# Routed experts of a token tower: each expert's last two tiles as one group of 256 rows

## The chip, the cores and the metric

One core of a Trainium2 chip runs the whole kernel in one launch. The metric is the device time of one execution in microseconds. The kernel before takes 499.87 us (median of 3 runs, 499.44 to 500.29). In one expert's work TensorE (PE) multiplies, ScalarE (ACT) applies GELU and rounds, VectorE (DVE) gates and forms remainders, GpSimd (POOL) issues indirect transfers, and SyncE (SP) issues plain ones.

## The reference, cut to what matters

2048 tokens pass an embedding MLP (256 to 1024 to 256), a two-layer gated recurrence, and a mixture of experts with one shared expert and eight routed ones. Only the last stage is changed in earnest:

```python
def geglu(x, w1, w2, w3):
    return jax.nn.gelu(x @ w1, approximate=False) * (x @ w2) @ w3
B, T, C = x.shape                       # 2048 rows of 256, experts 256 -> 1024 -> 256
xf = x.reshape(-1, C)
shared = geglu(xf, w1s, w2s, w3s)
logits = xf @ Wg
idx = jnp.argmax(logits, axis=-1)
final = jnp.zeros_like(xf)
for e in range(N_EXPERTS):              # 8
    y = geglu(xf, W1[e], W2[e], W3[e])
    final = final + jnp.where((idx == e)[:, None], y, 0.0)
return (shared + final).reshape(B, T, C)
```

With the inputs drawn for this case the argmax sends 144, 240, 444, 241, 337, 200, 293 and 149 tokens to experts 0 to 7 (worked out from the reference itself). In tiles of 128 rows that is 2, 2, 4, 2, 3, 2, 3 and 2, so 20 tiles.

## The kernel before, in words

Every product is made from three: each fp32 operand is split into a rounded high part and the low remainder, and `mm3` (L248 to L252) issues high by high, high by low and low by high. The high part is an ACT copy, the low part a DVE subtraction that waits for it.

The program is one instruction stream for each engine, written out by hand and tied by semaphores. Chunks c = 0 to 31 are the embedding MLP, with the recurrence's units between them; c = 32 to 55 are the first three quarters of the shared expert, in which the router's logits are made (`router_logits`, L598), the rows are ranked, and scattered by expert into `x_sorted` in DRAM (16 indirect transfers, L416). Then come the routed tiles, and c = 56 to 63, the last quarter of the shared expert, with the fetch of the routed rows, the sums and the output.

A routed tile (`routed_tile`, PE L726) is 128 rows. PE turns the 256 columns of the tile (`row_transposes`), then keeps the rows in the array (xTp is the stationary operand) and streams 512 columns of w1 or w2 past them (`up_half`, 24 products). ACT makes GELU, DVE gates into g_buf; both are rows by hidden columns, so PE has to turn them in 8 transposes (`g_transposes`, L719) before the 24 down products of 256 columns. One tile's down products run behind the next one's up products. The expert of a tile is read from a table (`expert_of`, a register load). PE runs 16 tiles in any case (SURE) and up to 7 more in `Fori(SURE, END)` with an `If` (L756, L757), since the number of tiles depends on the routing. When a tile is the first of its expert, ACT and DVE split the next expert's weights during it: three pairs `next_hi` (L948) and `next_lo` (L1348) of 2048 columns each.

POOL stores each finished tile with one indirect transfer (`to_tokens`, L422), each of which waits until the one before has landed. Its loop always has XT = 23 rounds; the rounds past the last real tile store rows that go to a spare place of `y_tokens`. Nothing waits for these but POOL itself, and the program is over when all engines are.

SP zeroes `x_sorted` in 25 transfers (L304) and loads the weights.

Of the kernel before, what the change touches and what calls it, by code (L numbers as in the profile page):

```python
# [5 lines left out]
P = 128  # L6
# [13 lines left out]
def build(nc, idx, codebook, tok_w1, tok_b1, tok_w2, tok_b2, gru_wz, gru_bz, gru_wh, gru_bh,  # L20
# [3 lines left out]
    KD = D // P  # L24
# [9 lines left out]
    XT = TILES + EXPERTS - 1  # L34
    SURE = TILES
    END = XT
# [30 lines left out]
    LOG = {43: 3}  # L67
    LOG_END = {31: 0, 38: 1, 41: 2}
# [10 lines left out]
    x_sorted = nc.dram_tensor("x_sorted", [(XT + 2) * P, D + 1], F32, kind="Internal").ap()  # L79
    y_tokens = nc.dram_tensor("y_tokens", [(TILES + 1) * P, D], F32, kind="Internal").ap()  # L80

    with ExitStack() as ctx:
# [25 lines left out]
        r_qT = region(8)  # L108
        r_stage = region(28)
        r_xh = region(8)  # L110
        r_rows = region(17)
        r_xl = region(4)
        r_xb = region(8)
        r_gelub = region(2)

# [33 lines left out]
        x_row = at("x_row", [P, D], F32, r_xl)  # L149
        y_row = at("y_row", [P, D], F32, r_xl + K)  # L150
        xTp = at("xTp", [P, 2, KD, P], F32R, r_xl + 2 * K)
# [20 lines left out]
        wgs = small("wgs", [P, KD, EXPERTS])  # L172
# [21 lines left out]
        tile_no = small("tile_no", [P, XT, EXPERTS - 1])  # L194
        past = small("past", [P, XT, EXPERTS - 1])
        expert_f = small("expert_f", [P, XT])
        turns = small("turns", [P, END + 1], U16)
        fresh = small("fresh", [P, XT])
# [37 lines left out]
        logit_ps = sem("logit_ps"); logits_taken = sem("logits_taken"); onehot_steps = sem("onehot_steps"); onehot_done = sem("onehot_done")  # L236
        rank_ps = sem("rank_ps"); router = sem("router"); placed = sem("placed"); routed = sem("routed"); scattered = sem("scattered")
        first_row_land = sem("first_row_land"); x_land = sem("x_land"); x_ps = sem("x_ps"); xT_hi = sem("xT_hi"); xT_lo = sem("xT_lo")
        a_ps = sem("a_ps"); b_ps = sem("b_ps"); gelu_done = sem("gelu_done"); g_done = sem("g_done")
        gT_ps = sem("gT_ps"); gT_hi = sem("gT_hi"); gT_lo = sem("gT_lo")  # L240
        tile_done = sem("tile_done"); y_taken = sem("y_taken"); y_stored = sem("y_stored")
        act_turn = sem("act_turn"); fetch_land = [sem(f"fetch_land{b}") for b in range(BLOCKS)]
# [15 lines left out]
        def back_of(engine):  # L258

            engine.wait_ge(routed, 1)  # L260
            return engine.value_load(turns[0:1, END:END + 1], min_val=0, max_val=END - SURE) + SURE

# [18 lines left out]
        def _(sp):  # L281
# [5 lines left out]
            sp.dma_start(wgs[:], wg).then_inc(small_land, 16)  # L287
# [15 lines left out]
            with sp.Fori(0, XT + 2) as j:  # L303
                sp.dma_start(x_sorted[bass.ds(j * P, P), :], zero_row[:]).then_inc(zeroed, 16)  # L304
# [13 lines left out]
            sp.dma_start(x_row[:], x_sorted[0:P, 0:D]).then_inc(first_row_land, 16)  # L318
# [22 lines left out]
            sp.wait_ge(x_land, back * 16 + 16)  # L341
# [14 lines left out]
        def _(pool):  # L356
# [5 lines left out]
            def gather(b):  # L362
                for i in range(BT):
# [13 lines left out]
            pool.wait_ge(pool_const, 4)  # L377
            pool.affine_select(out=before[:], in_=before[:], compare_op=ALU.is_gt, fill=0.0, base=0,
# [4 lines left out]
                      allow_small_or_imprecise_dtypes=True).then_inc(pool_const, 1)  # L383
            pool.iota(tile_no[:], [[1, XT], [0, EXPERTS - 1]], base=0, channel_multiplier=0,
# [36 lines left out]
            def to_tokens(i):  # L421
                pool.indirect_dma_start(  # L422
                    out=y_tokens, out_offset=bass.IndirectOffsetOnAxis(ap=row_ids[:, i:i + 1].bitcast(I32), axis=0),
                    in_=y_row[:], in_offset=None,
# [4 lines left out]
            for i in range(XT):  # L429
                pool.wait_ge(y_taken, i + 1)  # L430
                if i:
                    pool.wait_ge(y_stored, i * 16)
                to_tokens(i)
# [3 lines left out]
        def _(pe):  # L437
# [160 lines left out]
            def router_logits(b):  # L598
# [5 lines left out]
                for i in range(BT):  # L604
                    for k in range(KD):
                        last = pe.matmul(ps[:, FLIP, i * EXPERTS:(i + 1) * EXPERTS], xlT[:, k, i * P:(i + 1) * P],  # L606
                                         wgs[:, k, :], start=(k == 0), stop=(k == KD - 1))
                last.then_inc(logit_ps, 1)

# [8 lines left out]
            def row_transposes(i):  # L618
                if isinstance(i, int) and i == 0:
                    pe.wait_ge(first_row_land, 16)  # L620
                else:
                    pe.wait_ge(x_land, i * 16)
# [829 lines left out]
```

## Time and profile before

| what | value |
|---|---|
| median of 3 runs | 499.87 us |
| the profiled execution | 499.71 us, of which the span of its instructions is 498.0 us |
| PE busy | 490.6 us (99%) |
| DVE busy | 320.2 us (64%) |
| ACT busy | 248.6 us (50%) |
| POOL busy | 71.2 us (14%) |
| first routed up product | 269.56 us |
| last real store of routed rows issued | 465.65 us |

The time outside the span is 499.71 - 498.0 = 1.7 us. A record of a busy engine shows how long its instruction was in flight; since matmuls overlap, what one costs is the distance between starts. Idle time is shown only in front of an instruction, with what ended it. Register and branch instructions are not busy time, but the trace has them by line, as PEldq, ACTq or DVEq.

### The profile page before, as it was taken

How to read it: one execution, taken by the hardware profiler on the slowest of the kernel's cores; microseconds unless marked ns; L12 is line 12 of the kernel's file. 1: busy time of each engine (PE TensorE's matmuls, PEld its weight loads, DVE VectorE, ACT ScalarE, POOL GpSimd, SP SyncE). 2: the span in 40 equal slices, each digit the busy share in tenths (PEclk: the TensorE clock that was granted, in tenths of full speed). 3: DMA queues.
4: the chain of work that ended last, by engine and by line, in shares of the span. 5: the costliest groups of instructions: out<-in, count | busy, mean ns of one | idle time of the engine just before them, and what ended most of it. 6: DMA issues, size and time to landing. Idle time of an engine off the chain costs nothing.

```text
span 498.0 us, 9330 instructions
## 1 busy us (share of the span) xinstructions
PE 490.6 (99%) x2946; PEld 434.0 (87%) x2947; DVE 320.2 (64%) x533; ACT 248.6 (50%) x380; POOL 71.2 (14%) x85
## 2 busy tenths in 40 slices
PE   8999999999999999999999999999999999999997
PEld 7889888888888888988888898898898898898886
DVE  2567768668676778657635866833857477557364
ACT  3776774575653553433433765534554457254321
POOL 4431031011011001103460001011001000101110
PEclk9999999999999999999999999999999999999999
DMA  4999010000000004000454465620546084500352
GB/s 132 325 295 239 7 42 1 1 0 2 1 1 1 1 0 168 3 0 33 138 169 108 155 222 205 201 105 32 195 167 227 21 265 133 193 32 32 108 189 84
DMA packets 22857, 52.70 MB, mean 106 GB/s; under 512 B 6096, under 2 KB 16336, under 8 KB 18864
## 3 DMA queue, kind: packets, MB, share of 16 engines
q1 hardware_dynamic: 17168, 42.39, 26.1%
q0 software_dynamic: 2640, 7.22, 4.0%
q10 hardware_dynamic: 3024, 2.75, 1.8%
q8 instruction: 16, 0.26, 0.2%
q14 instruction: 9, 0.07, 0.0%
HBM read 41.85 MB, written 10.51 MB: 105 GB/s over the span
## 4 chain that ended last, share of the span: by engine, by line
PE 94%; DVE 3%; issue 1%; ACT 1%; DVEq 0%
PE ps L250 28%; PE ps L251 28%; PE ps L252 28%; PE ps L719 4%; PE ps L440 2%; PE ps L606 1%; PE ps L624 1%; PE ps L548 1%; PE ps L595 1%; PE ps L583 1%; DVE stats L1080 1%; DVE v_gate L1111 0%; ACT a_gate L867 0%; ACT t_gate L865 0%; ACT v_gate L869 0%
## 5 line engine op out<-in xcount | busy, mean ns | idle before, releaser
L1015 DVE TENSOR_TENSOR hT<-ps,hT 128x512 fp32r<-128x512 f32 x64 | 43.9, 686 | 34.9 <-ACT hT L818 16.6
L1348 DVE TENSOR_TENSOR w_slots<-stage,w_slots 128x2048 f32 x24 | 54.8, 2287 | 15.2 <-ACT w_slots L948 15.1
L250 PE MATMUL ps<-w_slots,xTp 128*128 (+1 forms) x160 | 64.2, 401 | 0.2
L252 PE MATMUL ps<-w_slots,xTp 128*128 (+1 forms) x160 | 62.5, 391 | 0.0
L251 PE MATMUL ps<-w_slots,xTp 128*128 (+1 forms) x160 | 62.2, 389 | 0.0
L422 POOL DMA_INDIRECT y_tokens<-y_row,row_ids x23 | 22.4, 975 | 198.9 <-DVE y_row L1371 188.4
L250 PE MATMUL ps<-w_slots,gTp 128*128 (+1 forms) x160 | 46.8, 293 | 0.0
L818 ACT ACTIVATE hT<-ps 128x512 fp32r<-128x512 f32 x32 | 19.1, 598 | 54.1 <-DVE ps L1021 48.4
L252 PE MATMUL ps<-w_slots,gTp 128*128 (+1 forms) x160 | 45.3, 283 | 0.0
L251 PE MATMUL ps<-w_slots,gTp 128*128 (+1 forms) x160 | 45.2, 283 | 0.0
L1329 DVE TENSOR_TENSOR g_buf<-ps,gelu_buf 128x512 f32<-128x512 f32 x40 | 26.8, 685 | 28.1 <-PE ps L252 28.1
L948 ACT ACTIVATE w_slots<-stage 128x2048 f32 x21 | 40.3, 1917 | 3.9 <-issue 3.9
L1021 DVE TENSOR_TENSOR ps<-ps,gelub 128x512 f32<-128x512 f32 x32 | 22.3, 697 | 30.9 <-PE ps L252 26.0
L972 ACT ACTIVATE gTp<-ps 128x512 fp32r<-128x512 f32 x40 | 21.7, 595 | 39.0 <-PE ps L719 39.0
L802 ACT ACTIVATE ps<-ps,b 128x512 f32<-128x512 f32 x32 | 21.1, 660 | 36.1 <-PE ps L252 36.0
L964 ACT ACTIVATE gelu_buf<-ps 128x512 f32<-128x512 f32 x40 | 23.9, 597 | 29.7 <-PE ps L252 25.3
L814 ACT ACTIVATE gelub<-ps 128x512 f32<-128x512 f32 x32 | 19.2, 600 | 37.5 <-PE ps L252 36.6
L250 PE MATMUL ps<-w2p,hT 128*128 128x256 f32 x128 | 36.8, 288 | 1.0 <-DVE hT L1015 0.7
L250 PE MATMUL ps<-w_slots,hT 128*128 128x256 f32 x128 | 36.5, 285 | 0.0
L252 PE MATMUL ps<-w_slots,hT 128*128 128x256 f32 x128 | 36.2, 283 | 0.0
L251 PE MATMUL ps<-w_slots,hT 128*128 128x256 f32 x128 | 36.2, 283 | 0.0
L252 PE MATMUL ps<-w2p,hT 128*128 128x256 f32 x128 | 36.2, 283 | 0.0
(183 smaller groups left out, 1289.5 us busy)
## 6 DMA issues: line engine op xcount, KB each, us to landing
stage<-ew_in SPq DMA_DIRECT2D x24, 1024.0 KB, 5.0
x_sorted<-zero_row SPq DMA_DIRECT2D x25, 128.5 KB
x_row<-x_sorted ACTq DMA_DIRECT2D x21, 128.0 KB
stage<-w1s_in SPq DMA_DIRECT2D x2, 1024.0 KB, 8.9
fetched<-y_tokens SPq DMA_DIRECT2D x4, 512.0 KB, 5.3
out_rows<-fetched SPq DMA_DIRECT2D x3, 512.0 KB
first_stage<-tok_w_in SPq DMA_DIRECT2D x1, 1024.0 KB, 4.9
first_stage<-tok_w_in SPq DMA_DIRECT2D x4, 256.0 KB
```

What stands on the lines that cost most here:

```text
L250: pe.matmul(dst, lhs_hi, rhs_hi, start=start, stop=False, skip_group_check=shares_bank)
L251: pe.matmul(dst, lhs_hi, rhs_lo, start=False, stop=False, skip_group_check=shares_bank)
L252: return pe.matmul(dst, lhs_lo, rhs_hi, start=False, stop=stop, skip_group_check=shares_bank)
L422: pool.indirect_dma_start(out=y_tokens, out_offset=bass.IndirectOffsetOnAxis(ap=row_ids[:, i:i + 1].bitcast(I32), axis=0), in_=y_row[:], i ...
L802: act.activation(bank, bank, ACT.Gelu_apprx_tanh, bias=b1[:, c % HC:c % HC + 1]).then_inc(h_gelu, 1)
L948: act.activation(w_slots[:, bass.ds((e & 1) * SLOT + c * WCH, WCH)], stage[:, c, :], ACT.Copy).then_inc(split_hi, 1)
L964: act.activation(gelu_buf[:, n, :], ps[:, 2 * n, :], ACT.Gelu).then_inc(gelu_done, 1)
L972: act.activation(gTp[:, 0, n * BT:(n + 1) * BT, :].rearrange("p c n -> p (c n)"), ps[:, 4 + n, :], ACT.Copy).then_inc(gT_hi, 1)
L1015: dve.tensor_tensor(hT[:, c % RING, 1, :], ps[:, bank, :], f32(hT[:, c % RING, 0, :]), ALU.subtract).then_inc(h_lo, 1)
L1021: dve.tensor_tensor(bank, bank, gelub[:], ALU.mult).then_inc(s_gated, 1)
L1329: dve.tensor_tensor(g_buf[:, n * NB:(n + 1) * NB], ps[:, 2 * n + 1, :], gelu_buf[:, n, :], ALU.mult).then_inc(g_done, 1)
L1348: dve.tensor_tensor(w_slots[:, bass.ds(to + (PART + c * WCH), WCH)], stage[:, c, :], f32(w_slots[:, bass.ds(to + c * WCH, WCH)]), ALU.subt ...
```

## The change: what it does

Each expert's last two tiles (one or both possibly part empty) become a window of 256 rows. In a window the weights are loaded into the array and the 256 rows stream past them (`window_up`, four steps p of 24 products of 256 columns), so that the hidden values come out already turned, and the 8 transposes for each tile go. Tiles ahead of the window, the singles, are worked as before, inside the expert's turn, behind the window's first step. Down products of high rows take the high and the low part of w3 in one product of 512 columns, into two halves of a bank, which DVE adds (`take_tile`, a reduction, in place of the copy); so a tile's down has 8 products of 512 and 8 of 256 columns.

```diff
-    XT = TILES + EXPERTS - 1
+    WINDOW = 2 * P
+    PAIRS = HC // 2
+    MORE = TILES - 2
+    XT = 2 * EXPERTS + MORE
...
-            with sp.Fori(0, XT + 2) as j:
-                sp.dma_start(x_sorted[bass.ds(j * P, P), :], zero_row[:]).then_inc(zeroed, 16)
+            for j in range(XT + 2):
+                sp.wait_ge(h_lo, HC + j * 3 // 4)
+                sp.dma_start(x_sorted[j * P:(j + 1) * P, :], zero_row[:]).then_inc(zeroed, 16)
...
             for i in range(XT):
-                pool.wait_ge(y_taken, i + 1)
+                pool.wait_ge(y_taken, i + 2)
                 if i:
                     pool.wait_ge(y_stored, i * 16)
+                pool.sem_inc(y_free, 1)
                 to_tokens(i)
...
+            def expert(e, odd):
+                count = singles_of(pe, e)
+                s = ahead_of(pe, e)
+                last = last_of(pe, e)
+                pe.wait_ge(split_lo, e * 3 + 5)
+                pe.wait_ge(pair_lo, e + 1)
+                window_up(e, 0, odd)
+                if isinstance(e, int) and e == 0:
+                    chunk_down(AHEAD - 1, 0)
+                    pe.wait_ge(acc_taken, 2 * (2 * BLOCKS - 1))
+                else:
+                    window_down(e * PAIRS, PAIRS - 1, not odd)
+                with pe.If(count > 0):
+                    pe.wait_ge(one_lo, s + e + 1)
+                    single_half(s, 0, odd)
+                    pe.wait_ge(w_lo, e * PAIRS + 1)
+                    single_half(s, 1, odd)
+                    pe.wait_ge(y_taken, s + e * 2 + 1)
+                    one_transposes(s + e + 1)
+                    with pe.Fori(1, MORE) as j:
+                        with pe.If((count - j) > 0):
+                            single_turn(s + j - 1, 0)
+                            ...
+                            single_down(s + j - 1, odd)
+                    single_turn(last, 0)
+                window_up(e, 1, odd)
+                with pe.If(count > 0):
+                    single_turn(last, 1)
+                pe.wait_ge(w_lo, e * PAIRS + 1)
+                window_up(e, 2, odd)
+                pe.wait_ge(one_lo, s + count + e + 1)
+                pair_transposes(e + 1)
+                with pe.If(count > 0):
+                    ...
+                    single_down(last, odd)
+                ...
+                window_down(e * PAIRS + 1, 0, odd)
+                pe.wait_ge(w_lo, e * PAIRS + 2)
+                window_up(e, 3, odd)
+                window_down(e * PAIRS + 2, 1, odd)
+                pe.wait_ge(pair_lo, e + 2)
+                one_transposes(s + count + e + 1)
+                window_down(e * PAIRS + 3, 2, odd)
+
+            pe.wait_ge(pair_lo, 1)
+            one_transposes(0)
             chunk_down(AHEAD - 2, 0)
...
+            def take_tile(done, bank, count=1):
+                dve.wait_ge(tile_done, done)
+                dve.wait_ge(y_free, done)
+                dve.tensor_reduce(y_rows[:, bass.ds(((done + 1) & 1) * D, D)], ps[:, bank, :].rearrange("p (h n) -> p n h", h=2), AX,
+                                  ALU.add).then_inc(y_taken, count)
```

ACT and DVE have an `expert` in the same order, with the same `Fori(1, MORE)` and `If`. On DVE one without singles is: gate 0, the two takes, remainder 0, `next_lo` 0, gate 1, remainder 1, `next_lo` 1, gate 2, remainder 2, the remainder of the next window's rows, gate 3, remainder 3, that of the next single's rows, `next_lo` 2. Window rows and single rows are read ahead into x_pair and x_one. The router's logits are now made with wg in the array (32 columns) and the rows streaming, four tiles side by side in the array's column groups, and turned back by one transpose; and `turns` holds five small tables in place of one entry for each tile.

The loop that leaves tiles out stands on PE before in this form (order of the program; L757 is the `If`, and the rows left out are its body):

```order
L756 UNCONDITIONAL_BRANCH
L756 ISA
L757 COMPARE_AND_BRANCH
...
L757 UNCONDITIONAL_BRANCH
L756 REGISTER_ALU
L756 COMPARE_AND_BRANCH
```

and now inside every expert with singles, between the turning of the next single's rows and the turning of the last single's hidden values:

```order
L683 MATMUL ps<-ident,x_one 128x128 x2
L839 UNCONDITIONAL_BRANCH
L839 ISA
L840 COMPARE_AND_BRANCH
...
L840 UNCONDITIONAL_BRANCH
L839 REGISTER_ALU
L839 COMPARE_AND_BRANCH
```

The same three rows drive a round; the loop of before had 7 rounds once in a program, the one of now has 13 in each expert that has a single.

The end of POOL's stream, before:

```order
L395 TENSOR_SCALAR veps<-mv 128x4
L397 TENSOR_TENSOR rstd<-veps,mhalf 128x4
L409 IOTA xn_73 128x16
L416 DMA x_sorted<-xn_73,pos 3200x257 x16
L422 DMA y_tokens<-y_row,row_ids 2176x256 x23
```

and now:

```order
L440 TENSOR_SCALAR veps<-mv 128x4
L442 TENSOR_TENSOR rstd<-veps,mhalf 128x4
L454 IOTA xn_73 128x16
L461 DMA x_sorted<-xn_73,pos 5888x257 x16
L467 DMA y_tokens<-y_rows,row_ids 2176x256 x30
```

Seven stores more stand at the end of the stream; with 20 real tiles 3 of 23 were spare, and 10 of 30 are.

## Rows read from the trace of the kernel before

**Rows 1.** The page: busy time and chain by engine.
```profile
PE 490.6 (99%) x2946; PEld 434.0 (87%) x2947; DVE 320.2 (64%) x533; ACT 248.6 (50%) x380; POOL 71.2 (14%) x85
...
PE 94%; DVE 3%; issue 1%; ACT 1%; DVEq 0%
```

**Rows 2.** Timeline of PE, one routed tile: start us, duration us, line, operation, count.
```profile
343.60 1.04 PE L719 MATMUL ps<-ident,g_buf 128*128 128x128 f32 x8
344.39 0.47 PE L250 MATMUL ps<-w_slots,xTp 128*128 x1
...
349.95 0.38 PE L624 MATMUL ps<-ident,x_row 128*128 128x128 f32 x2
350.08 0.36 PE L250 MATMUL ps<-w_slots,gTp 128*128 x1
...
353.04 0.49 PE L719 MATMUL ps<-ident,g_buf 128*128 128x128 f32 x3
```

**Rows 3.** Timeline of ACT and DVE, splitting the next expert's weights.
```profile
346.55 1.91 ACT L948 ACTIVATE w_slots<-stage 128x2048 f32 x1
...
348.72 2.29 DVE L1348 TENSOR_TENSOR w_slots<-stage,w_slots 128x2048 f32 x1 [0.54 <-ACT w_slots L948]
350.93 0.68 DVE L1329 TENSOR_TENSOR g_buf<-ps,gelu_buf 128x512 f32<-128x512 f32 x1
351.53 0.41 DVE L1149 TENSOR_TENSOR xTp<-ps,xTp 128x256 fp32r<-128x256 f32 x1
```

**Rows 4.** Timeline of DVE and ACT, one chunk of the shared expert.
```profile
478.17 0.70 DVE L1021 TENSOR_TENSOR ps<-ps,gelub 128x512 f32<-128x512 f32 x1 [0.99 <-PE ps L252]
...
478.90 0.60 ACT L818 ACTIVATE hT<-ps 128x512 fp32r<-128x512 f32 x1 [1.57 <-DVE ps L1021]
...
479.53 0.69 DVE L1015 TENSOR_TENSOR hT<-ps,hT 128x512 fp32r<-128x512 f32 x1 [0.66 <-ACT hT L818]
```

**Rows 5.** PE's register loads of the table, 300 to 440 us: ns min/median/max, first and last start.
```profile
L724 PEldq TENSOR_LOAD <-turns x29: 283/284/424, 304.2 to 436.6; - x29
```

**Rows 6.** Timelines of PE and DVE where the routed tiles begin.
```profile
269.56 0.47 PE L250 MATMUL ps<-w_slots,xTp 128*128 128x512 f32 x1
...
269.05 0.42 DVE L1149 TENSOR_TENSOR xTp<-ps,xTp 128x256 fp32r<-128x256 f32 x1
...
273.28 1.41 DVE L1058 TENSOR_TENSOR res<-ps,res 128x512 f32<-128x512 f32 x2
```

**Rows 7.** PE's loop over left-out tiles, 454 to 458 us: ns, first and last start.
```profile
L756 PEldq COMPARE_BRANCH  x4: 76/208/222, 454.8 to 457.3; - x4
...
L757 PEldq COMPARE_BRANCH  x3: 208/208/208, 455.3 to 456.9; - x3
```

**Rows 8.** Timeline of PE's products at the same place.
```profile
456.76 0.28 PE L252 MATMUL ps<-w_slots,gTp 128*128 x1
457.51 1.09 PE L719 MATMUL ps<-ident,g_buf 128*128 128x128 f32 x8 [0.47 <-issue]
```

**Rows 9.** Timeline of PE at the program's start.
```profile
1.25 7.19 PE L440 MATMUL ps<-zero_row 128*128 128x256 f32 x20 [1.25 <-DVE zero_row L991]
...
9.16 1.03 PE L440 MATMUL ps<-zero_row 128*128 128x256 f32 x4
```

**Rows 10.** Timelines of POOL and SP at the end.
```profile
465.65 0.97 POOL L422 DMA_INDIRECT y_tokens<-y_row,row_ids  x1 [6.29 <-DVE y_row L1371]
468.87 0.98 POOL L422 DMA_INDIRECT y_tokens<-y_row,row_ids  x1 [2.24 <-DMA y_tokens<-y_row,row_ids]
475.87 0.97 POOL L422 DMA_INDIRECT y_tokens<-y_row,row_ids  x1 [6.03 <-DMA y_tokens<-y_row,row_ids]
...
468.05 2.04 SPq L339 DMA_DIRECT2D fetched<-y_tokens  x4
```

**Rows 11.** PE's logit products of one block, and its longest waits in all.
```profile
L606 PE MATMUL ps<-wgs,xlT x16: 170/256/256, 188.1 to 189.7; 128*128 128x8 f32 x16
...
PE ps L250 <- issue: 0.9, 1, 0.9
```

More of the change, by code:

```diff
@@ L702, in up_half, with single_turn, single_down @@
                     last.then_inc(done, 1)
-            def down(i, slot):
+            def single_turn(s, n):
+                pe.wait_ge(g_done, s * 2 + (n + 1))
+                for c in range(HC // NH):
+                    j = n * (HC // NH) + c
+                    last = pe.transpose(ps[:, 4 + n, c * P:(c + 1) * P], g_buf[:, j * P:(j + 1) * P], ident[:])
+                last.then_inc(gT_ps, 1)
+            def single_down(s, odd):
+                side = 0 if odd else 1
                 for c in range(HC):
@@ L712, in down @@
+                    last = pe.matmul(ps[:, 7, 0:D], gTp[:, 1, c, :], w_slots[:, side * SLOT + o:side * SLOT + o + D],
+                                     start=False, stop=c == HC - 1, skip_group_check=True)
                 last.then_inc(tile_done, 1)
-            def g_transposes(i):
-                for n in range(NH):
-                    pe.wait_ge(g_done, 2 * i + n + 1)
-                    for c in range(HC // NH):
-                        j = n * (HC // NH) + c
-                        last = pe.transpose(ps[:, 4 + n, c * P:(c + 1) * P], g_buf[:, j * P:(j + 1) * P], ident[:])
-                    last.then_inc(gT_ps, 1)
@@ L976, in _, with window_gelu @@
-            act.wait_ge(routed, 1)
-            tile(0, second_hi)
-            with act.Fori(1, SURE) as i:
-                routed_tile(i)
-            back = back_of(act)
-            with act.Fori(SURE, END) as i:
-                with act.If((back - i) > 0):
-                    routed_tile(i)
+                    window_rows_hi(0, 0)
+                    single_rows_hi(0)
+            def window_gelu(e, p):
+                act.wait_ge(wa_ps, e * PAIRS + (p + 1))
+                act.activation(gelub[:], ps[:, p % 2 * 2, :], ACT.Gelu).then_inc(w_gelu, 1)
@@ L984, in _ @@
+            act.wait_ge(routed, 1)
+            expert(0, 0)
+            with act.Fori(0, EXPERTS // 2 - 1) as i:
+                expert(i * 2 + 1, 1)
+                expert(i * 2 + 2, 0)
+            expert(EXPERTS - 1, 1)
             for c in range(AHEAD, ALL):
@@ L1339, in routed_tile @@
[L1339 to L1352 removed]
+                    window_rows_lo(0, 0)
@@ new lines, in expert @@
+                window_gated(e, 1)
+                window_lo(e, 1)
+                with dve.If(count > 0):
+                    single_lo(last, 1)
+                next_lo(e, 1, odd)
+                window_gated(e, 2)
+                window_lo(e, 2)
+                window_rows_lo(e + 1, 1 - odd)
+                with dve.If(count > 0):
+                    take_tile(s + count + e * 2, 7)
+                window_gated(e, 3)
+                window_lo(e, 3)
+                single_rows_lo(s + count + e + 1)
@@ L1378, in _ @@
+                next_lo(e, 2, odd)
+            dve.wait_ge(routed, 1)
+            expert(0, 0)
+            with dve.Fori(0, EXPERTS // 2 - 1) as i:
+                expert(i * 2 + 1, 1)
+                expert(i * 2 + 2, 0)
+            expert(EXPERTS - 1, 1)
             back = back_of(dve)
-            with dve.Fori(SURE, END) as i:
-                with dve.If((back - i) > 0):
-                    routed_tile(i, lambda: take_routed(i - 1, 16 * i - 16))
             def finish(b):
```

453 lines of the change are left out of this document (271 added, 182 removed).

## The prediction

> **What bounds the kernel now.** I read the page first: PE is busy 99% of the span and carries 94% of the chain that ended last [rows 1]. So every instruction taken off PE is time, as long as PE finds work in its place, and every new wait of PE is time lost. I then read PE's timeline through one routed tile for the distances between starts, ACT's and DVE's for the steps between two of PE's groups, and last the sequencer's own rows (loops, register loads) and POOL's stream at the end, since the change touches both.
>
> A routed tile goes from 343.60 to 353.04, which is 9.44 us: 8 transposes in 0.79, 24 up products of 512 columns in 5.56 (0.08 of it a seam, so 0.228 each), 2 transposes of rows in 0.13, and 24 down products of 256 columns in 2.96, or 0.12 each [rows 2]. There is no idle time in it.
>
> **The work on the array.** A window is two tiles. Its up products are 4 steps of 24 with 256 columns: 96 x 0.12 = 11.5 us, against 2 x 5.56 = 11.1 before. Its down products are 16 pairs of 512 and 256 columns: 16 x (0.228 + 0.12) = 5.6, against 5.9. Six row transposes at 0.1 are 0.6, a seam or two 0.1. Sum 17.8 against 18.9: 1.1 saved, since 1.6 of transposes go. Eight windows save 8.7, and the four singles 0.1 each through the fused down product. Total **-9**. Were the 256-column products dearer with weights in the array, this would shrink; the down products of before have the same shape and bound it.
>
> **Loops that leave tiles out.** This is the largest term. Experts 2, 4 and 6 have 2, 1 and 1 singles. In each, PE passes Fori(1, 14): 13 rounds, of which 12, 13 and 13 do nothing. The kernel before has the same three driving rows, and left out three rounds at the end: the If's taken branch stands at 455.3 and, two rounds later, at 456.9, so one empty round takes 0.8 us of PE's sequencer; the taken branches alone are 0.208 and about 0.21 [rows 7]. Three rounds and the exit took about 2.7 us, and the array stood still from 456.88 to 457.51, 0.63, because the sequencer had been 2.1 us ahead (its loop end at 454.8, the last queued product at 456.76 + 0.12) [rows 7, 8]. That cover is all there is. So 13 rounds are 10.4 us of sequencer and 12 are 9.6, in all 30.4; less 2.1 ahead in expert 2, and less about 1.4 in experts 4 and 6, where the sequencer has just waited for x_one to land, 25.5 us remain. **+25.5**; between 20 (a full lead and rounds of 0.7) and 31 (no lead). ACT and DVE pass the same loop with branches of their own while PE stands, so theirs lies beside it.
>
> The Trainium skill, Advanced Engine Details and Errata, Control Flow Timing, gives some 108 ns for a compare and branch; by it a round of two would be near 0.4 and the term about 12. Rows 7 show 208 ns for a taken one and 0.8 for the round, and the measurement decides.
>
> **The clock behind these gaps.** PE then stands idle for 7 to 9 us three times, which no stretch of before shows; its longest waits are below 1.5. What the trace shows is the start, before which PE did nothing: 20 products begin at 1.25 and the next group at about 8.3, 0.35 each, where the later ones stand (1.03 - 0.38) / 3 = 0.22 apart [rows 9]. The idle start cost 20 x (0.352 - 0.217) = 2.7 us. I take 2.4 for each gap, **+7**, with 0 and 8 as ends. The Trainium skill, TensorE: Matmul & The Clock Gate, Part 1, says that an idle array falls to 1.2 GHz and returns to 2.4 GHz under load; no row of before shows it after a gap in the middle.
>
> **The chain through ACT and DVE.** For an expert without singles (0, 1, 3, 5, 7) I laid the steps in order. Gate to ACT's copy is 0.73, copy to remainder 0.63, remainder 0.69 [rows 4]; ACT's weight copy to DVE's start 2.17, that one's length to the next start 2.21, a 512-column step 0.60 [rows 3]. From gate 0 at 0: two takes, remainder 0 at 2.2, weights 3.4 to 5.6, gate 1 5.6, remainder 1 7.0, weights 9.0 to 11.2, gate 2, remainder 2 12.6, window rows 13.2 to 13.9, gate 3 about 15.3, remainder 3 16.8, weights 17.4 to 19.6. PE needs 17.8 for the same expert, and wants the next window's rows 13.3 after the end of its first up step. So it waits 0.7 the first time, and in expert 1, which follows another without singles, 1.5 to 2. Behind such a wait the sequencer is no longer ahead, and an expert starts with three table loads in a row, each 0.28 for the load itself [rows 5] and, an estimate, twice that with the register steps behind it: 1.9 against 1.4 of queued products, about 1 us more with the waits. Experts 1, 3, 5, 7: 4.3 of waits for rows less what the load gaps give DVE back, 4 of loads. **+7**; ends 1 and 12. The reduction in take_tile is in no row; a 512-column DVE step of 0.69 [rows 4] and the 256-column one of 0.41 [rows 3] bound it, I take the first, since it reads 512.
>
> **The start of the stage.** Before, PE's first routed product starts at 269.56, when the row remainder (269.05 + 0.42) is just done; ahead of it lies chunk_down(54), 12 x 0.12 = 1.4, so that began at about 268.0 [rows 2, 6]. Now one_transposes(0) stands ahead of chunk_down(54) and waits for the window's rows, 512 columns, so until 269.05 + 0.69 = 269.75: 1.7 us, and behind it come the table loads, 1.8 uncovered. In expert 0 PE also waits for DVE's two sums of res after chunk_down(55), 1.41 [rows 6] and 0.3 to be seen, which another half of up products covered before. **+5**; 2 to 7.
>
> **Small edits.** The logits of a block are 16 products in 1.7 us [rows 11]; now 16 of other shape and one transpose. Between a quarter of it and the same: 0 to -5 in all four blocks. Spreading the zeroing takes DMA load away near 18 to 40 us; PE's longest wait without a cause shown is 0.9 [rows 11]. DVE's copies lie beside PE's down products. Together **-1**, from -5 to +2.
>
> **The end.** POOL's 20 real stores are followed by 10 spare ones instead of 3. A store follows the one before after 3.22 us (465.65 to 468.87), and the one that meets the fetch of 2 MB, issued at 468.05, after 7.0, 3.8 more [rows 10]. Before, the last real one stood 498.0 - 465.65 = 32.35 before the end. Call E the time at which PE's chain would end the span. Now the last two tiles are taken together; relative to the rest of PE's work the first store comes about 0.7 later, at E - 31.6, and eleven more follow: -31.6 + 11 x 3.25 + 3.8 + 0.97 = 9. With something for the output transfers of 512 KB it meets, POOL ends the program at E + 10. **+10**; 6 to 14. Before this chain was covered by the last quarter of the shared expert; with 3 spare ones the last began one interval behind 475.87, near 479.
>
> **Sum.** 498.0 - 9 + 25.5 + 7 + 7 + 5 - 1 = 532.5 for E, 542.5 with the end, 544.2 with the 1.7 outside the span. The profiled execution (499.71) is 0.16 below the median of the runs, so 544.
>
> **Rivals.**
> 1. The clock stays at 2.4 GHz through the gaps: 537. For it: the page never shows less than 9 tenths. Against: the start at half pace. It decides if the products right behind a gap stand 0.12 apart.
> 2. Empty rounds are cheap inside an expert, because the body left out is passed without the long branch, or PE's queue hides them. Then term and clock go: 544 - 32.5 = 511. Against: the rows are the same three and rows 7 have three of three rounds at 208.
> 3. Code has to be fetched again: the body of two experts is far longer than a tile's, and five experts jump over the singles' code. The Trainium skill, Runtime: NRT & Kernel Launch, Instruction fetch mechanics, says a taken branch out of the fetched pages stalls. By rows, the nearest is 0.9, the longest wait of PE without a shown cause [rows 11]; two back jumps and fifteen skips at 0 to 0.9 are up to 15: 552 in the middle.
> 4. The other side, faster: the only thing that counts is the array's work. If PE's sequencer stays far enough ahead that rounds, loads and DVE's chain are all hidden, E is 498 - 9 - 1 = 488, and it becomes faster once POOL's spare stores also cost under 10, as they would if one spare store took 2.3 us in place of 3.22 (E + 0): 490. It decides from a lead of 10 us where rows 7 and 8 show 2.1.
> 5. Spare stores end inside the shared quarter: 534.
>
> **Chances.** Forecast 544: 0.44; rival 1 0.16; rival 2 0.07; rival 3 0.18; rival 5 0.1; rival 4 0.03; the rest, 0.02, ends within 0.2% by chance of signs. A measurement of this kernel tells 0.2% from no change. Range 524 to 560: it holds the forecast with most of its terms' ends, rivals 1, 3 and 5, and leaves out 2 and 4. Slower 0.95, same 0.01, faster 0.04.
>
> **What would show it.** In the profile after: PE idle before the first turn of g_buf behind the inner loop, three times, 7 to 10 us each, with COMPARE_BRANCH rows 0.8 apart; products behind it 0.21 apart for some us; PE waiting for the remainder of xW in experts 1, 3, 5 and 7, and none in 2, 4 and 6; POOL's last store behind the last output sum by about 10 us, and the chain that ended last running through POOL. I am wrong if PE stays above 95% busy, if POOL's last store starts before the last product, or if an expert of two tiles takes clearly more than 20 us.

## The result, and the profile after

The changed kernel takes 545.32 us (median of 4 runs, 544.43 to 546.14) against 499.65 before (498.76 to 500.29) on the same chip: ratio 1.0918, 95% interval 1.0894 to 1.0941. Slower by 9%, at the predicted place (544). The profiled execution has a span of 544.0, where before had 498.0.

The page after: the first line is busy time by engine, the second the granted TensorE clock in 40 slices, the last the chain that ended last. They answer to [rows 1].

```profile
PE 486.6 (89%) x3066; PEld 432.9 (80%) x3067; DVE 332.0 (61%) x540; ACT 248.7 (46%) x381; POOL 76.7 (14%) x91
...
PEclk9999999999999999999999997999699988999985
...
POOLq L93 0%; DMA y_tokens<-y_rows,row_ids 0%; POOLq L467 0%
```

PE has 4 us less of work in flight, but its share of the span fell from 99% to 89%. The clock, 9 in every slice before, dips to 7 and 6, and the end of the program belongs to POOL and no longer to PE (the view takes in only a few us of this chain, so its shares are near 0%). The list of PE's longest waits (line waited with, what ended the wait, us in all, times, longest):

```profile
PE ps L801 <- issue: 24.5, 3, 9.3
PE ps L683 <- DVE xW L1300: 3.3, 5, 1.6
PE ps L271 <- issue: 3.0, 5, 0.8
PE ps L271 <- DVE res L1209: 1.4, 1, 1.4
```

The longest wait of before was 1.3, at the program's start. L801 is the transpose of g_buf behind the inner loop: three waits, one in each expert with singles. PE's sequencer in the first of them, 320 to 340 us (ns min/median/max, first and last start), answers to [rows 7]:

```profile
L839 PEldq COMPARE_BRANCH  x13: 76/208/226, 325.3 to 334.2; - x13
L839 PEldq FUSED_REGOPS  x12: 39/39/51, 325.6 to 333.7; - x12
...
L840 PEldq COMPARE_BRANCH  x12: 208/208/215, 325.7 to 333.8; - x12
```

Twelve taken `If`s start between 325.7 and 333.8: eleven distances of 0.74 us. The loop's last branch starts at 334.2 and the turn behind it at 334.43, so it is PE's own sequencer that the array waits for. The timeline of PE at the same place, and its busy time and clock in stretches there and behind the second loop (columns of the second fence: stretch, length, busy time of PE, PEld, DVE, ACT and POOL with instructions, PEclk, DMA share, GB/s):

```profile
328.10 0.28 PE L812 MATMUL ps<-w_slots,gTp 128*128 128x256 f32 x1
334.43 1.11 PE L801 MATMUL ps<-ident,g_buf 128*128 128x128 f32 x4 [6.05 <-issue]
335.19 0.56 PE L271 MATMUL ps<-xW,w_slots 128*128 128x256 f32 x1
335.55 0.41 PE L272 MATMUL ps<-xW,w_slots 128*128 128x256 f32 x1
335.76 0.41 PE L273 MATMUL ps<-xW,w_slots 128*128 128x256 f32 x1
335.97 0.41 PE L271 MATMUL ps<-xW,w_slots 128*128 128x256 f32 x1
```

```profile
325.00:330.00 5.00, 3.37 (x20) 2.64 (x18) 1.71 (x3) 0.39 (x1) 0.00 (x0) 1.00 0.00 0
330.00:335.00 5.00, 0.57 (x3) 0.58 (x4) 0.00 (x0) 0.00 (x0) 0.97 (x1) 0.61 0.06 26
335.00:340.00 5.00, 5.00 (x33) 5.00 (x32) 1.06 (x2) 1.19 (x2) 0.00 (x0) 0.70 0.12 30
...
390.00:395.00 5.00, 2.04 (x10) 2.05 (x11) 0.26 (x1) 0.60 (x1) 0.00 (x0) 0.50 0.00 0
```

Behind the gap twelve products stand 0.21 apart instead of 0.12, the pace of the lower level of 1.2 GHz, and the granted clock of that stretch is 0.70, a mean over both levels. POOL's last stores and its closing row (the second fence is by line) answer to [rows 10]:

```profile
495.74 0.97 POOL L467 DMA_INDIRECT y_tokens<-y_rows,row_ids  x1 [15.68 <-DVE y_rows L1527]
498.96 0.97 POOL L467 DMA_INDIRECT y_tokens<-y_rows,row_ids  x1 [2.24 <-DMA y_tokens<-y_rows,row_ids]
502.17 0.97 POOL L467 DMA_INDIRECT y_tokens<-y_rows,row_ids  x1 [2.24 <-DMA y_tokens<-y_rows,row_ids]
509.05 1.59 POOL L467 DMA_INDIRECT y_tokens<-y_rows,row_ids  x1 [5.91 <-DMA y_tokens<-y_rows,row_ids]
...
537.68 0.97 POOL L467 DMA_INDIRECT y_tokens<-y_rows,row_ids  x1 [2.25 <-issue]
```

```profile
L93 POOLq DRAIN  x1: 6340/6340/6340, 537.5 to 537.5; - x1
```

The last product starts at 523.08. Before, it started at 494.63 and the span ended 3.3 after it, so PE's chain would have ended near 526.4, and POOL holds the program for 17.6 us more: stores until 537.68, and a drain of 6.34 at the end of its stream. The kernel before has this closing row too, but it begins at 478.9 and is over 10 us ahead of the last product:

```profile
L82 POOLq DRAIN  x1: 5772/5772/5772, 478.9 to 478.9; - x1
```

### The profile page after: what moved, and what is told of

Read it like the earlier page. It is cut to its first block and busy times, and to the rows that moved or that the text cites. A ratio compares the mean times of both kernels' runs of the same rounds, so it can differ in the third digit from the quotient of the medians.

```text
span 544.0 us, 8965 instructions
## 1 busy us (share of the span) xinstructions
PE 486.6 (89%) x3066; PEld 432.9 (80%) x3067; DVE 332.0 (61%) x540; ACT 248.7 (46%) x381; POOL 76.7 (14%) x91
## 5 line engine op out<-in xcount | busy, mean ns | idle before, releaser
L271 PE MATMUL ps<-xW,w_slots 128*128 128x256 f32 x256 | 75.2, 294 | 4.5 <-issue 3.0
L272 PE MATMUL ps<-xW,w_slots 128*128 128x256 f32 x256 | 73.8, 288 | 0.0
L273 PE MATMUL ps<-xW,w_slots 128*128 128x256 f32 x256 | 73.8, 288 | 0.0
L467 POOL DMA_INDIRECT y_tokens<-y_rows,row_ids x30 | 29.8, 993 | 253.4 <-DVE y_rows L1527 196.1
L1166 DVE TENSOR_TENSOR hT<-ps,hT 128x512 fp32r<-128x512 f32 x64 | 43.9, 685 | 34.6 <-ACT hT L928 17.6
L1506 DVE TENSOR_TENSOR w_slots<-stage,w_slots 128x2048 fp32r<-128x2048 f32 x24 | 54.9, 2289 | 9.4 <-ACT w_slots L1075 9.2
L271 PEld LDWEIGHTS ps<-xW,w_slots 128*128 128x128 f32 x256 | 50.7, 198 | 6.8 <-issue 6.0
L272 PEld LDWEIGHTS ps<-xW,w_slots 128*128 128x128 f32 x256 | 50.5, 197 | 0.0
L273 PEld LDWEIGHTS ps<-xW,w_slots 128*128 128x128 f32 x256 | 50.3, 196 | 0.0
L780 PE MATMUL ps<-w_slots,hW 128*128 128x512 f32 x128 | 47.6, 406 | 0.0
L1075 ACT ACTIVATE w_slots<-stage 128x2048 fp32r<-128x2048 f32 x24 | 45.9, 1911 | 0.0
L1066 ACT ACTIVATE hW<-ps 128x512 fp32r<-128x512 f32 x32 | 19.1, 598 | 53.0 <-DVE ps L1497 53.0
L1497 DVE TENSOR_TENSOR ps<-ps,gelub 128x512 f32<-128x512 f32 x32 | 22.3, 697 | 29.9 <-PE ps L273 17.6
L271 PE MATMUL ps<-w2p,hT 128*128 128x256 f32 x128 | 36.9, 288 | 1.0 <-DVE w2p L1177 0.7
L272 PE MATMUL ps<-w2p,hT 128*128 128x256 f32 x128 | 36.2, 283 | 0.0
L273 PE MATMUL ps<-w2p,hT 128*128 128x256 f32 x128 | 36.2, 283 | 0.0
L1172 DVE TENSOR_TENSOR ps<-ps,gelub 128x512 f32<-128x512 f32 x32 | 22.3, 697 | 22.4 <-PE ps L273 22.3
```

The costliest lines, as they stand in the source:

```text
L271: pe.matmul(dst, lhs_hi, rhs_hi, start=start, stop=False, skip_group_check=shares_bank)
L272: pe.matmul(dst, lhs_hi, rhs_lo, start=False, stop=False, skip_group_check=shares_bank)
L273: return pe.matmul(dst, lhs_lo, rhs_hi, start=False, stop=stop, skip_group_check=shares_bank)
L467: pool.indirect_dma_start(out=y_tokens, out_offset=bass.IndirectOffsetOnAxis(ap=row_ids[:, i:i + 1].bitcast(I32), axis=0), in_=y_rows[:, i ...
L780: pe.matmul(ps[:, 4 + i, :].rearrange("p (h n) -> p h n", h=2), hW[:, p, 0, cols], w_parts[:, side, :, o:o + D], start=p == 0 and c == 0, ...
L1075: act.activation(w_slots[:, o:o + WCH], stage[:, c, :], ACT.Copy).then_inc(split_hi, 1)
```

## The experiments

The line numbers differ a little between the kernels: DVE's rows remainder of a window is L1300 in the changed kernel and L1307 where POOL's loop was edited.

**Loop bound.** e1_count_loop lets the inner loop end at the expert's count, on PE, ACT and DVE:

```diff
-                    with pe.Fori(1, MORE) as j:
+                    with pe.Fori(1, count) as j:
```

> The changed kernel with the inner loop of the singles ended at the expert's own count (1 or 2) instead of 14, on PE, ACT and DVE, so at most one empty round is left in an expert. My theory (empty rounds take PE's sequencer 0.73 us each, 9.4 us in three experts, and the array restarts at half pace behind each): the three idle gaps of 6.3, 9.5 and 9.5 us in front of L801 shrink to under 0.5 each, the products behind them stand 0.12 apart and not 0.17, and PE's last product comes 24 + 5 = 29 us sooner, at 494. POOL's twelve stores start 29 us sooner too, so the time falls by the same: 516. Rival (the gaps are waits for DVE's or ACT's work in the singles, which the profile puts down to issue): the gaps stay at 5 us or more and the time stays above 530. Rival (a gap is only moved: DVE becomes late in experts 2, 4 and 6 once PE no longer stands): 520 to 525, with new waits of PE for a remainder there.

Measured 517.01, ratio to before 1.0364 (1.0340 to 1.0387), 28.3 less than the changed kernel. The last product moves from 523.08 to 493.85, 29.2 sooner. The turn of g_buf behind the loop comes without an idle time shown:

```profile
328.92 0.60 PE L801 MATMUL ps<-ident,g_buf 128*128 128x128 f32 x4
```

So the loops and the clock behind them are 28 to 29 us together.

**Spare stores.** e2_no_spare_stores puts the stores past SURE under a condition:

```diff
+            stored = back_of(pool)
+            for i in range(SURE, XT):
+                with pool.If((stored - i) > 0):
+                    store(i)
```

> The changed kernel with POOL's spare stores, those past the last real tile, left out by a condition (none is issued; the loops on PE are untouched). My theory (the 10 spare stores and POOL's closing drain of 6.3 us set the end): the program ends 3.4 us behind the last product as in the kernel before, at a span of 526.7 and a time of 528. Rival (the end is set by the output transfers, which the spare stores only delay): 535 to 545. Rival (the drain is 6.3 us wherever it stands, but begins early enough to be hidden): the same 528, and the drain is seen near 500 in the profile.

Measured 529.37, ratio 1.0603 (1.0586 to 1.0621), 16.0 less. POOL's last store and its drain, in the profile by timeline and by line:

```profile
500.19 0.97 POOL L467 DMA_INDIRECT y_tokens<-y_rows,row_ids  x1 [2.24 <-DMA y_tokens<-y_rows,row_ids]
```

```profile
L93 POOLq DRAIN  x1: 4327/4327/4327, 502.5 to 502.5; - x1
```

The drain is there too, but lies beside the shared quarter, since it begins at 502.5. It is shorter, but it also begins later behind the last store, and it ends 6.6 us after that store's start, against 6.1 in the changed kernel.

**Both.** e3_both has the two edits.

> Both edits together: loops ended at the count and no spare stores. If the two terms are independent and my sizes hold: 528 - 29 = 499, within 0.5% of the kernel before (499.7), so that the windows' saving on the array (about 9 us and the 3 us before the stage) is then spent on waits for window rows, table loads and the start of the stage, about 11. If the windows themselves were slower than tiles the result would lie above 508; if they save all that the array's count says, with no new wait, at 488.

Measured 499.91, ratio 1.0016 (1.0005 to 1.0028). Against the changed kernel 45.4 us go, and 28.3 + 16.0 = 44.3 is the sum of the parts: the two costs are separate, and together they are the whole loss. What is left is a kernel that saves array work and gives all of it away elsewhere.

**Busy gap.** e4_busy_gap keeps the changed kernel's loop and adds two products of 256 columns to every round on PE, outside the `If`, into bank 5, whose contents are then not needed; they are extra work and change no output.

```diff
+                        for _ in range(2):
+                            pe.matmul(ps[:, 5, 0:D], ident[:], b2r[:], start=True, stop=True, skip_group_check=True)
```

> The changed kernel with two products of 256 columns put into every round of PE's inner loop (their result is thrown away), so that the array works while the sequencer passes the empty rounds; nothing else changes. My theory (the half pace behind a gap comes from the idle time, not from the first use of other weights or from reading cold code): the 24 up products behind the loop stand 0.12 apart, not 0.17, and the four turns ahead of them 0.11, not 0.23; the granted clock stays at 1.00 in these stretches. Each round grows from 0.73 to about 0.95 by the products (2 x 0.43), so the time is 545 + 39 x 0.2 - 5 = 548. Rival (it is not the idle time): the pitch stays at 0.17, and the time is 553.

Measured 553.82 (one run). PE at the same place as above:

```profile
329.30 10.52 PE L841 MATMUL ps<-b2r,ident 128*128 128x256 f32 x48
339.66 0.60 PE L801 MATMUL ps<-ident,g_buf 128*128 128x128 f32 x4
340.01 0.36 PE L271 MATMUL ps<-xW,w_slots 128*128 128x256 f32 x1
340.22 0.28 PE L272 MATMUL ps<-xW,w_slots 128*128 128x256 f32 x1
340.33 0.28 PE L273 MATMUL ps<-xW,w_slots 128*128 128x256 f32 x1
```

The four turns take 0.60 instead of 1.11 and the products behind stand 0.12 apart: with the array busy through the loop there is no slow stretch, and the granted clock of these stretches is 1.00. So it is the array's idleness that costs the clock. The time itself was 6 off my number, and more than half of that is the round, which grew to 1.05 and not to 0.95 (39 rounds). It is still PE's sequencer that sets it. Its rows in expert 4, by line, with the `If` now L842:

```profile
L842 PEldq COMPARE_BRANCH  x13: 208/208/213, 386.0 to 398.6; - x13
```

These start 1.05 apart. The trace records each extra product twice (48 records in the fence above are the 24 products of expert 2's twelve empty rounds), and records stand 0.216 apart where the array is never short of work, so a round's four need 0.86 of the array. Another 1.0 is a wait of PE at 34.67 that the profile of the changed kernel does not have; the rest stays open.

**Zeroing.** e5_zero_burst is e3_both with the transfers that zero `x_sorted` issued at once, as before the change:

```diff
             for j in range(XT + 2):
-                sp.wait_ge(h_lo, HC + j * 3 // 4)
```

> As e3_both, but the 32 transfers that zero x_sorted go out one behind the other again, as in the kernel before, instead of spread over chunks 8 to 31. The kernel before idles 0.93 us near 34.2 us in front of chunk 4's up products without a cause in the profile; with the spread this gap is gone. My theory (code or weights came late behind the burst): the gap of about 0.9 us near 33 to 36 us is back, and the last product comes 0.9 later than 494.6. Rival (the gap went for another reason): no gap there, the same end.

Measured 500.8 (one run), span 498.7 against 497.8. Between 18 and 74 us no two products of PE start more than 0.5 us apart in either, and 0.6 of the 0.9 had passed by 17 us, at the program's start; the spans of e3_both's own runs lie between 496.8 and 499.1. The spread of the zeroing is worth nothing that this shows. Before, PE waited 0.93 us at 35.13. That wait is gone in the changed kernel and the burst does not bring it back, but e4_busy_gap, where the zeroing is spread, has one of 1.01 at 34.67. So it does not follow the zeroing, and its cause stays open.

**Rows earlier.** e6_rows_earlier is e3_both with the next window's rows (`window_rows_hi`, `window_rows_lo`) ahead of the weight split 1, so that PE need not wait for them:

```diff
+                window_rows_lo(e + 1, 1 - odd)
                 next_lo(e, 1, odd)
                 window_gated(e, 2)
                 window_lo(e, 2)
-                window_rows_lo(e + 1, 1 - odd)
```

> As e3_both, but ACT's and DVE's two steps on the next window's rows stand before the second weight split (next_hi 1, next_lo 1) instead of behind the third chunk. My theory (PE's waits for xW in experts 1, 3, 5 and 7 come from the 5 us of split and chunk ahead of that step, and the uncovered table loads, 0.9 each, come from these waits): the four gaps of 0.62 and 1.02 in front of L690 and the four of 1.04 in front of the next first up step shrink below 0.3, 5.5 us less: 494.4, ratio 0.990. Rival (ACT and DVE need 19.6 us for an expert whatever the order, so the wait only moves, to a chunk's remainder or the next split): at most 2 us less, 498, with new waits of PE for DVE's hW or w_slots.

A miss: 504.22, ratio 1.0105 (1.0084 to 1.0126), some 4 us slower than e3_both. In the timeline of PE at the end of expert 1:

```profile
309.28 0.50 PE L787 MATMUL ps<-w_slots,hW 128*128 128x512 f32 x1 [0.87 <-DVE hW L1508]
...
311.76 0.35 PE L271 MATMUL ps<-xW,w_slots 128*128 128x256 f32 x1 [0.82 <-issue]
```

The wait for rows is gone, and a longer one for remainder 2 stands one step of 8 products later, with the table loads behind it bare as before. The period of an expert of two tiles (from its first product to the next one's) rose from 19.3 to 19.9, and expert 0's from 19.7 to 21.8, which is another 2 us of the loss. All that DVE does here hangs on one chain, and I had only changed which link is last.

**Loads later.** e7_loads_later is e3_both with PE's three table loads behind the first `window_down`:

```diff
-                count = singles_of(pe, e)
...
                     window_down(e * PAIRS, PAIRS - 1, not odd)
+                count = singles_of(pe, e)
```

> As e3_both, but PE's three table loads stand behind the first up step and the down products that follow, where 32 products are queued, instead of at the expert's head. My theory: the gaps of 1.04 us (four) and 0.5 to 0.8 (two) in front of an expert's first up step shrink to 0.15, 4.5 us less in all if the waits for xW stay as they are; but DVE has this much less time, so the waits for xW grow by about half of it: 497.5, ratio 0.995. Rival (all of it is given back to DVE's chain): 499.9.

A miss again: 504.68, ratio 1.0107 (1.0086 to 1.0127). Where I had looked, it works: the period of an expert of two tiles is 18.4, 0.9 less. It is paid for twice elsewhere, as the timeline of PE in expert 0 and in expert 4 shows:

```profile
277.06 0.58 PE L271 MATMUL ps<-xW,w_slots 128*128 128x256 f32 x1 [4.00 <-issue]
...
379.78 0.44 PE L690 MATMUL ps<-ident,x_one 128*128 128x128 f32 x2 [1.54 <-DMA x_one<-x_sorted]
```

In expert 0 the loads now stand behind the wait for DVE's sums of res, so 2.5 us of them are bare, and a gap of 4.0 brings the half pace with it (products 0.21 apart behind it). In expert 4 PE is ready for the next single's rows 4.9 us after ACT issued their transfer, and they landed 6.5 after it; in e3_both both were 5.5.

**All orders.** e8_all_orders has both of these and, at the start of the stage, `chunk_down(54)` ahead of `one_transposes(0)` and the wait for the sums of res put off until their banks are overwritten.

```diff
+            chunk_down(AHEAD - 2, 0)
             pe.wait_ge(pair_lo, 1)
             one_transposes(0)
-            chunk_down(AHEAD - 2, 0)
```

> As e3_both with both of these orders, and at the stage's start the first single's rows turned behind chunk_down(54) and not ahead of it, and PE's wait for the two sums of res moved behind two further up steps. By my theory the array then has only its own work: 499.9 less 5.5 (rows), less 1.3 (loads at the start), less 1.8 and 1.4 (start): 490, ratio 0.981, faster than the kernel before. Rival (ACT's and DVE's 19.6 us an expert bind where two experts without singles follow each other): one wait of about 2 us in expert 1, 492.

Measured 502.6, ratio 1.0065 (1.0051 to 1.0079): 2 us better than either, from the start, but the wait for remainder 2 (PE's waits: 4.6 us in five) is still there.

**The link itself.** After three misses I read DVE and ACT in e3_both in order of time instead of PE's waits, for expert 1. First DVE, then ACT:

```profile
298.92 0.69 DVE L1508 TENSOR_TENSOR hW<-ps,hW 128x512 fp32r<-128x512 f32 x1 [0.67 <-ACT hW L1073]
300.72 2.29 DVE L1513 TENSOR_TENSOR w_slots<-stage,w_slots 128x2048 fp32r<-128x2048 f32 x1 [1.11 <-ACT w_slots L1082]
302.93 0.69 DVE L1504 TENSOR_TENSOR ps<-ps,gelub 128x512 f32<-128x512 f32 x1
304.29 0.69 DVE L1508 TENSOR_TENSOR hW<-ps,hW 128x512 fp32r<-128x512 f32 x1 [0.67 <-ACT hW L1073]
304.90 0.68 DVE L1307 TENSOR_TENSOR xW<-ps,xW 128x512 fp32r<-128x512 f32 x1
```

```profile
298.29 0.60 ACT L1073 ACTIVATE hW<-ps 128x512 fp32r<-128x512 f32 x1 [2.48 <-DVE ps L1504]
298.78 1.91 ACT L1082 ACTIVATE w_slots<-stage 128x2048 fp32r<-128x2048 f32 x1
```

ACT idles 2.48 for a gate of DVE, then makes the weight copy, and DVE idles 1.11 for that. The copy needs nothing of the gate. e9_copy_earlier is e3_both with one line moved on ACT:

```diff
                 window_gelu(e, 1)
+                next_hi(e, 1, odd)
                 window_hi(e, 1)
                 with act.If(count > 0):
                     single_hi(last, 1)
-                next_hi(e, 1, odd)
```

> Taken from e3_both, with one move on ACT: the weight copy next_hi(e, 1) stands between window_gelu(e, 1) and window_hi(e, 1), where ACT is idle for 2.48 us in e3_both (298.29, waiting for DVE's gate), in place of behind window_hi(e, 1). DVE's order is as it was. Theory A (the chain runs through ACT's copy: DVE idles 1.11 us for it at 300.72, then weights, gate 2, remainder 2 and the window's rows follow without slack): DVE's wait of 1.11 goes, the rows' remainder is done 1.1 us earlier, PE's wait of 0.62 for xW goes in experts 1, 3, 5 and 7, and, since the sequencer is ahead again, the gap at the table loads falls from 1.04 to about 0.5, as it was behind expert 0. The period of an expert of two tiles falls from 19.3 to 18.2 or so; four of them give 4 to 4.5 us off 499.9: 495.6. Rival B (any shift in this chain only moves the wait, as in e6_rows_earlier where it went from the rows to remainder 2 and grew by 0.5; or the copy waits for its weights to land): 499.9 to 502.

Measured 494.01, ratio 0.9909 (0.9876 to 0.9941), span 491.7: 1.6 under its number, and faster than before by 0.9%. DVE and PE at the same place:

```profile
299.46 2.29 DVE L1513 TENSOR_TENSOR w_slots<-stage,w_slots 128x2048 fp32r<-128x2048 f32 x1
301.67 0.69 DVE L1504 TENSOR_TENSOR ps<-ps,gelub 128x512 f32<-128x512 f32 x1
303.02 0.69 DVE L1508 TENSOR_TENSOR hW<-ps,hW 128x512 fp32r<-128x512 f32 x1 [0.66 <-ACT hW L1073]
303.63 0.68 DVE L1307 TENSOR_TENSOR xW<-ps,xW 128x512 fp32r<-128x512 f32 x1
```

```profile
305.12 0.38 PE L690 MATMUL ps<-ident,x_one 128*128 128x128 f32 x2
```

The wait of DVE is gone, the rows' remainder is 1.3 earlier, PE turns the next single's rows without waiting, and, ahead again, hides most of the table loads (0.4 left of 1.04). The period fell from 19.3 to 18.1.

**Start.** e10_start is e9_copy_earlier with PE's order at the start of the stage changed (the same two moves as in e8, and expert 0's table loads ahead of `chunk_down(54)`):

```diff
+            pe.wait_ge(routed, 1)
+            table = singles_of(pe, 0), ahead_of(pe, 0), last_of(pe, 0)
+            chunk_down(AHEAD - 2, 0)
             pe.wait_ge(pair_lo, 1)
             one_transposes(0)
-            chunk_down(AHEAD - 2, 0)
-            pe.wait_ge(routed, 1)
```

> Taken from e9_copy_earlier, with the start of the stage reordered on PE alone: the three table loads of expert 0 stand ahead of chunk_down(54), that one ahead of one_transposes(0), and the wait for DVE's sums of res (acc_taken) is put off from window_up(0, 1) to the first product that overwrites their banks. Theory A (the start's gaps are order, not work): in e9_copy_earlier PE stands 1.84 us before one_transposes (265.31 to 267.15) and 0.80 before the first routed product (269.53); chunk_down(54) fills 1.4 of the first, and the loads, 2.1 us from 267.32 to 269.43 on the sequencer, lie under queued products, so the first routed product comes at about 267.4, 2.1 earlier. The wait of 1.62 before window_up(0, 1) goes too. 3.7 off 494.0 in all, less up to 1 given back in expert 0's DVE chain (gate 0, two sums of res, remainder 0, weights): 490.8. Rival B (the chain through ACT and DVE sets expert 0's pace whatever PE's order; e8_all_orders gained 2.5 of gaps at the start and then waited 1.36 in expert 0): 492.5 to 494.

Measured 494.0, ratio 0.9898 (0.9868 to 0.9929): no difference from e9 that these four runs, 492.6 to 495.8, can tell. The first routed product comes 2.5 us earlier, expert 1 only 1.3. The timeline of ACT says why:

```profile
267.24 0.38 ACT L1029 ACTIVATE xTp<-ps 128x256 fp32r<-128x256 f32 x1 [1.45 <-PE ps L690]
269.98 2.08 ACTq L1105 DMA_DIRECT2D x_pair<-x_sorted  x1
272.11 0.60 ACT L1071 ACTIVATE gelub<-ps 128x512 f32<-128x512 f32 x1 [4.49 <-issue]
```

ACT reads its own four table entries and issues a transfer, 4.5 us in all, before the first GELU. e11_tables_first has this start too, reads the entries on ACT and DVE one step earlier, and ACT issues that transfer behind the GELU:

```diff
                     window_rows_hi(0, 0)
+                    act.wait_ge(routed, 1)
+                    table = singles_of(act, 0), ahead_of(act, 0), last_of(act, 0), window_behind(act, 0)
                     single_rows_hi(0)
```

> Taken from e10_start: ACT and DVE too read expert 0's table entries earlier, between the window rows and the single's rows of the chunk before (where both are idle from 266.6 to 267.3), and ACT issues expert 0's x_pair transfer behind gelu 0 instead of ahead of it. Theory A (in e10_start the first expert is held by ACT: its table loads run from 267.33 to 269.9 and the issue of the transfer takes 2.08 more, so gelu 0 starts at 272.20, 2.3 after PE's up step 0 has ended at 269.87, and everything in DVE behind it is late; PE then waits 1.18, 0.22, 0.58 and 1.04): gelu 0 starts near 269, gate 0 near 270.1, DVE's chain is 2.5 earlier, and these four gaps go but for seams: 2 to 2.5 off the 490.5 of e10_start's span, 488.2, time 491. Rival B (the loads ahead delay the single's rows or the last remainder, or other waits of the chain take over): span 490 or more, time 493 to 494.5.

Measured 491.81 (5 runs, 490.75 to 493.0), ratio 0.9839 (0.9824 to 0.9853). ACT:

```profile
268.91 0.60 ACT L1073 ACTIVATE gelub<-ps 128x512 f32<-128x512 f32 x1 [1.04 <-PE ps L273]
269.07 1.37 ACTq L1106 DMA_DIRECT2D x_pair<-x_sorted  x1
```

This is the best version: 1.6% faster than the kernel before, and its interval lies apart from that of e10. About 3 of these 8 us were won ahead of the routed tiles, by the small edits, and not by the windows.

## Why the prediction was right, point by point

The mechanisms were right, but that the time was (544 for 545.3) is luck: two errors offset each other. E, where PE's chain would end, was 6.1 too late (532.5 for 526.4), and the end 7.6 too short (10 for 17.6).

- **Array, -9.** Right. In e11_tables_first the period of experts 3 and 5 is 18.06, and its one gap that is more than a seam is a distance of 0.37 where 0.12 is usual, so 17.8 of work against 2 x 9.44 [rows 2]: 1.1 for each window, as I had worked out.
- **Loops, +25.5.** Right: the three waits in front of L801 are 24.5. A round is 0.74, where the one of before took 0.81 [rows 7]: the register operation between its two branches (FUSED_REGOPS) is 0.04 now and was 0.10. The lead of the sequencer at the loop was 3.0 in expert 2 and 0.2 in experts 4 and 6, 3.4 in all, where I had taken 4.9; the two errors nearly cancel. The rule of the Trainium skill (Advanced Engine Details and Errata, Control Flow Timing), some 108 ns for a compare and branch, does not hold here: 208 where taken, 76 where not. The rivals that made empty rounds cheap fall with it, and e1 shows the whole term.
- **Clock, +7.** The mechanism is right, the size too large: the 24 products behind the three gaps stood 0.176, 0.166 and 0.177 apart against 0.123, and the turns 0.23 against 0.11, so 1.6 for each gap on the mean and 4.8 in all. I had taken the start of the program, whose products stay slow longer: one distance of 0.59 and eleven of 0.43 before they stand 0.22 apart. e4 shows that idleness is the cause, so rival 1, the clock staying at 2.4 GHz, is out.
- **ACT and DVE, +7.** Right in place and nearly in size: PE waited 0.6 for rows in experts 1, 3 and 5 and 1.0 in expert 7, where I had 1.5 to 2 in expert 1, and stood 1.0 at the table loads behind experts 1, 3 and 5 and 0.5 ahead of expert 1; 6.5 together, as eight distances between starts, of which 0.12 each is usual. A wait of 1.1 in expert 4, of which 0.7 is put down to the transfer of the single's rows, was in no term. What I did not see is that my own step list had the cause in it: remainder 1 ends at 7.7, weights start at 9.0. That 1.3 of idle DVE was a line on ACT.
- **Start, +5.** 4.3, from gaps of 1.84, 0.80 and 1.70; the table loads cost 0.8 and not 1.8.
- **Small edits, -1.** Off by 2: what stands ahead of the stage came 3 us earlier. The logits gained most of it: their 16 products of a block now take 0.58 us to the next product's start, where they took 1.7 [rows 11], 4.5 in four blocks less new waits. 0.8 had come by 75 us, before any logits, since the wait of 0.93 is not there; e4 and e5 show that the spread of the zeroing is not what took it away. This gain is inside my range for the step (-5 to +2).
- **The end, +10.** The mis-sized term: 17.6. I had let the program end 0.97 after the last store's start. It took 6.1, because POOL's stream ends with a drain that is over 6.1 us after that start; what it waits for, no run shows (a store alone is followed by the next after 3.22). The kernel before has such a drain, but it is over at 484.6, under the shared quarter, so the chain of before does not have it and I had not read it there. Of the rest, 2.5 is a second slow store (5.8 to the next) beside the one that I counted (I had added 1 for it), while the output transfers that SP issued at 506.72 were under way, and 0.9 is that the first of the twelve stores came at 495.74 and not at 494.8. e2 takes off 16.0. Rival 5, spare stores that end inside the shared quarter, is out.
- **Rival 3, code fetched again.** No PE wait without a cause is above 0.8 outside the loops: nothing here shows it. The wait of 0.9 to 1.0 near 35 us, in the kernel before and in e4, has no cause shown and stays open.

In e6, e7 and e8 I was wrong three times with the same habit: I moved what PE waited for, and not what that one was waiting for.

## What to carry to other kernels

A loop with an `If` for work that may be absent costs a busy array its empty rounds, less the sequencer's lead, and the clock behind them too: end it at the count. Before an order is changed to take out a wait, follow it back through the engines to the first instruction that idles for something it does not need, and move that one; a gain in one expert is also to be read in those with other waits. Work at the end of a side engine's stream is hidden only while it and its closing drain end before the main engine does.

## What the runs showed of the hardware

- POOL's stream ends with a drain, in the kernel before too. It is over 6.1 us after the start of the last indirect store where spare stores end the stream (the changed kernel and e1_count_loop alike, the drain itself 6.34), 6.6 in e2 and e3 (4.33, but it begins later), and 5.5 in the kernel before (5.77). I had expected it to end with the store.
- A taken branch on PE is 208 ns and an empty round of `Fori` with `If` 0.74 us, 38 times; in the kernel before 0.81.
- Behind gaps of 6 to 9.5 us the array had half its pace for part of the next 24 products, 1.6 us each; behind a gap of 4 in e7 too (all 24 stood 0.216 apart), and there even behind a wait of 1.5 with 0.4 soon after it (the 24 products after it stood 0.181 apart). A single gap of 1.8 at the start of the stage did not. The same time filled with products kept it.
- A transfer with an address from a register held ACT for 1.4 to 2.4 us the first time, over all runs, and 0.4 in later experts.
